# The edge sum's loop on VectorE: 32 steps instead of 56, the last 24 in line, and block numbers read one word at a time

## The reference, cut to what matters

```python
agg  = segment_sum(x[src], dst, n)                  # and the degree of each node
x    = layernorm(x + relu([x, agg/deg] @ W_fc + b_fc) + x @ W_res + b_res)
conv = lambda h: (segment_sum(h[src] @ Wm + bm + edge_attr @ We + be, dst, n) + h @ Ws + bs)
x    = layernorm(x + conv2(relu(conv1(x))))
```

## Time and profile before

| | |
|---|---|
| median of three runs | 3635.19 us |
| profiled execution | 3643.39 us, of it 3641.6 us span |
| VectorE busy, whole span | 2379.0 us (65%) |
| TensorE busy, whole span | 3127.8 us (86%) |
| mark, line 930 | 728 times, 483 ns each |
| add, line 941 | 728 times, 279 ns each |

### The profile page before, as it was taken

How to read it: one execution, slowest core, us unless ns; L and a number is a source line. 1 busy time by engine, 2 the same in 40 slices (tenths; PEclk the granted TensorE clock), 3 DMA queues, 4 the chain that set the end, 5 groups by cost and what they waited for, 6 DMA issues and landing times.

```text
span 3641.6 us, 114539 instructions
## 1 busy us (share of the span) xinstructions
PE 3127.8 (86%) x38568; PEld 2925.0 (80%) x38568; DVE 2379.0 (65%) x6286; ACT 1579.8 (43%) x2164; POOL 2104.5 (58%) x2436
## 2 busy tenths in 40 slices
PE   0228999999999999788888888999999979999995
PEld 0127988888888888677777888999999879999995
DVE  8679998988888888687788664333333333333335
ACT  0123677778999899677777632000000210000000
POOL 5761345455666666333333227777777677777774
PEclk9869999999999999899999859999999999999998
DMA  3521445555666666577777517999999679999995
GB/s 90 136 19 54 181 184 210 205 223 217 246 244 236 237 249 247 192 220 212 208 215 217 155 61 291 399 381 389 397 386 398 236 294 400 385 384 398 390 389 225
DMA packets 234074, 928.58 MB, mean 255 GB/s; under 512 B 46723, under 2 KB 146193, under 8 KB 178030
## 3 DMA queue, kind: packets, MB, share of 16 engines
q1 hardware_dynamic: 182559, 846.33, 62.2%
q0 software_dynamic: 51392, 80.97, 7.7%
HBM read 676.56 MB, written 250.56 MB: 255 GB/s over the span
## 4 chain that ended last, share of the span: by engine, by line
PE 48%; POOL 16%; issue 15%; DVE 11%; DMA 6%; DVEq 3%; ACT 2%; ACTq 0%; POOLq 0%; SPq 0%
PE ps L1118 30%; POOL msg L1280 10%; PE ps L1141 7%; DVE union L814 5%; PE ps L1188 5%; DMA msg<-y_tab,idx 4%; POOL abuf L1222 3%; PE ps L1110 3%; DVE union L930 2%; ACT union L1428 1%; DVE abuf L941 1%; POOL union L1222 1%; PE ps L1197 1%; DVEq L469 1%; PE ps L1078 1%
## 5 line engine op out<-in xcount | busy, mean ns | idle before, releaser
L1280 POOL DMA_INDIRECT msg<-y_tab,idx x1512 | 1614.4, 1068 | 921.5 <-issue 456.4
L1118 PE MATMUL ps<-union,abuf 128*128 128x192 bf16 x14112 | 1210.7, 248 | 14.7 <-DVEq L785 10.2
L1118 PEld LDWEIGHTS ps<-union,abuf 128*128 128x128 f16 x14112 | 1177.4, 99 | 18.5 <-issue 10.6
L1410 ACT ACTIVATE abuf<-ps 128x784 f16<-128x784 f32 x1152 | 949.1, 824 | 262.1 <-PE ps L1141 237.2
L814 DVE TENSOR_TENSOR union<-lane,union 128x1568 f16<-128x1568 f16 (+1 forms) x1384 | 911.9, 710 | 8.4 <-PE ps L1141 4.7
L1118 PE MATMUL ps<-early,abuf 128*128 128x195 bf16 x7154 | 809.3, 249 | 0.0
L1118 PEld LDWEIGHTS ps<-early,abuf 128*128 128x128 f16 x7154 | 641.9, 99 | 92.1
L1141 PE MATMUL ps<-union 128*128 128x98 f16 (+2 forms) x4192 | 661.3, 287 | 57.4 <-DVE union L814 56.3
L1386 ACT ACTIVATE idx<-src_g 128x7 int32 (+1 forms) x216 | 44.4, 205 | 1258.8 <-PE ps L1110 1248.1
L1188 PE MATMUL ps<-union 128*64 128x128 f32 x7280 | 467.7, 287 | 92.6 <-ACT union L1428 89.9
L1188 PEld LDWEIGHTS ps<-union 128*64 128x64 f32 x7280 | 421.1, 144 | 139.3 <-DVE abuf L941 121.8
(11 more groups left out here) (231 smaller groups left out, 1386.5 us busy)
## 6 DMA issues: line engine op xcount, KB each, us to landing
abuf<-a_dram SPq DMA_DIRECT2D x288, 1568.0 KB
a_dram<-abuf SPq DMA_DIRECT2D x72, 3136.0 KB
union<-in_edge_attr_dram SPq DMA_DIRECT2D x728, 160.0 KB, 3.1
msg<-y_tab,idx POOLq DMA_INDIRECT x1512
y_tab<-union SPq DMA_DIRECT2D x28, 336.0 KB, 2.2
abuf<-in_x_dram SPq DMA_DIRECT2D x28, 224.0 KB, 3.6
y_tab<-early SPq DMA_DIRECT2D x7, 682.5 KB, 5.5
out_dram<-union SPq DMA_DIRECT2D x2, 800.0 KB, 3.5
```

Source lines behind the costliest of these rows:

```text
L1118: last = nc.tensor.matmul(ps[:, bank, 0:3 * width_of[r]], abuf[:, buffer, hi * P:(hi + 1) * P], ycols[r][:, hi, :], start=hi == 0, stop=hi ...
L1280: pool.indirect_dma_start(msg[:, s, 0:3 * width_of[r]], None, y_tab[r], bass.IndirectOffsetOnAxis(ap=idx[:, s:s + 1], axis=0)).then_inc(ga ...
L1410: A.activation(abuf[:, j, :].rearrange("p (h w d) -> p w h d", w=WPB, d=WD) [:, w:w + 2, :, :], ps[:, w % 4:w % 4 + 2, 0:WIN].rearrange("p ...
```

## The change

A new constant `HELD` = 4. The steps of the loop go into a function that is called twice: in a loop of 22 passes with 4 turns (32 steps), and once more, with constants in place of the loop's register, for the 3 turns (24 steps) that are left. Block numbers are loaded one word at a time, in every fourth step, and the load stands behind the mark of its step and ahead of the waits of the add, where before it stood ahead of the mark. Nothing on the other engines is edited; SyncE keeps its 56 steps in a pass.

```diff
+    HELD = 4
...
-                with dve.Fori(0, ESTEPS // EB, TURNS) as turn:
-                    for n in range(EB * TURNS):
+                def edge_steps(turn, turns):
+                    for n in range(EB * turns):
                         i, h = turn + n // EB, n % EB
-                        if n % (2 * EB) == 0:
-                            bs = load_blocks(turn * (EB // 4) + (first_block + n) // 4, min(2 * EB, EB * TURNS - n))
                         if h % 2 == 0:
                             dve.wait_ge(e_hot[h // 2], i + 1)
                         dve.wait_ge(e_rel[h], i + 1)
...
                         if h % 2:
                             marks.then_inc(e_mark[h // 2], 1)
+                        if n % 4 == 0:
+                            bs = load_blocks(turn * (EB // 4) + (first_block + n) // 4, 4)
                         b = (h - LAG) % EB
                         dve.wait_ge(e_mm[b], i + (2 if h >= LAG else 1))
                         dve.wait_ge(e_add, i * EB + (h + EB))
-                        to = flat(sums_e[:, bass.ds(bs[n % (2 * EB)], 1), :])
+                        to = flat(sums_e[:, bass.ds(bs[n % 4], 1), :])
                         V.tensor_tensor(to, to, ps[:, b, 0:P], ALU.add).then_inc(e_add, 1)
+
+                whole = ESTEPS // EB // HELD * HELD
+                with dve.Fori(0, whole, HELD) as turn:
+                    edge_steps(turn, HELD)
+                edge_steps(whole, ESTEPS // EB - whole)
```

## The result

The kernel after the change takes 3542.4 us (median of four runs: 3540.2, 3561.2, 3543.9, 3540.8) against 3635.8 us of the kernel before, measured beside it. The ratio is 0.9754, 95% interval 0.9721 to 0.9788: 93 us faster.

What follows compares the result with a forecast made beforehand. VectorE's sequencer was taken to bound the edge sum; 437 us of steps + 44 loads + 7.6 branches + 5 restart and stalls = 493.6 against 552.1, 58.5 less, giving 3576 us; range given 3546 to 3609.

Steps and rivals of the forecast that it cites:

- What bounds the kernel: Edge sum, 552.1 us: VectorE sets the pace at 0.60 us a step, and its own sequencer stops it for 115 us.
- The held loop: Edge loop on VectorE: about 210 instructions stay held, so 36 us of branch pauses go and 21 branches cost 7.6 us.
- restart and inner stalls: Edge sum: clock recovery after pauses, chain refilling and short issue stalls; 5 us of the 37 remain.
- The load term: Edge loop: 182 one-word loads between mark and add at 0.24 us each, 44 us against 42 before.
- Restart and the branch: Edge sum: 5 us kept for restart and inner stalls, 7.6 us for 21 branches at 0.36 us each.
- The sum: Edge sum: 437 + 44 + 7.6 + 5 = 493.6 us against 552.1, 58.5 less.
- Not held: Edge loop: the 32-step body is fetched again at 21 branches, 124 us in place of 5, kernel 3696 us; 7%.
- Load waits for the mark: Edge loop: each load waits until the mark is through, add 0.70 us late, 127 us, kernel 3660 us; 5%.
- Loads hidden: Edge loop: the mark covers the loads at no cost, stage 450 us, kernel 3533 us; 6%.
- What would show it: Edge sum: no 4 us idle ahead of marks, clock 1.00 from second pass, loaded steps 0.64 us mark to add, "issue" moved.

Runs made afterwards that it cites:

- the loop alone: Kernel before with only the 32-step loop, keeping the old loads of up to four words ahead of the mark: 3563.0 us, ratio 0.9801.
- the moved loop of 48: Changed kernel with 48 steps a pass (309 instructions) and the body's start shifted to another slot in the instruction stream: 3540.4 us, ratio 0.9750.
- the announced branch: Kernel before, 56 steps kept, with only the loop's branch target announced at the top of each pass: 3552.2 us, ratio 0.9782.
- the early address: Changed kernel with the address operation of the next load in the loop issued one step earlier: 3541.0 us, ratio 0.9734.
- the two kernels with the filler: 14 useless TensorE products added during the wait ahead of the fold: on the kernel before 3619.2 us, on the changed kernel 3541.5 us.
- load ahead of the mark: Changed kernel with its one-word loads moved from behind the mark to ahead of it: 3575.7 us, ratio 0.9837.
- loop of 40: Changed kernel with 40 steps a pass in place of 32 (258 instructions): 3557.3 us, ratio 0.9777.
- loop of 48: Changed kernel with 48 steps a pass in place of 32 (309 instructions), start not moved: 3628.1 us, ratio 0.9972.

## Why the prediction was right in kind and 34 us off

**What bounds the kernel**: right. VectorE's sequencer set the pace, through the load ahead of the mark and the pause at the branch. Both were tried alone, and each gave a gain.

**The held loop**: right. The forecast took 36 us of branches and 32 of restart and inner stalls off and put 7.6 back, 60.4 in all; the loop alone measured 57.5. That the pause is fetched code was argued from one other loop; the moved loop of 48 and the announced branch show it. The reason given, that 210 instructions are about what is held, was too coarse: 360 are held if they start at the right place, and 309 are not if they don't. (The counts of 209 and 291 that it compared were short, as it said; the trace has 244 in the first passes of line 828's loop and 340 in the edge loop.) The Trainium skill, Runtime: NRT & Kernel Launch, section Instruction fetch mechanics, has a branch out of the window of code stall the engine; here the trace agrees, with 3 us. Its pages of 256 instructions do not fit the stalls, which stand 128 apart, nor the five packets; the rule that the prediction drew from it, that a body which crosses a page is lost, does not hold either, since all bodies that are held cross the end of a block.

**The load term**: the step that failed. It was sized 0.24 us a load and measured 0.13. The terms in the sum were right, but the start was not. The chain of waits after, through the step with the load (start, length, what; DVEq is the sequencer):

```profile
1702.66 0.31 DVEq L470
1702.97 0.09 DVE union L929
...
1703.11 0.04 DVEq L942
...
1703.19 0.06 DVEq L942
...
1703.29 0.30 DVE abuf L942
```

The load begins at 1702.66, 0.10 *ahead* of its mark's start at 1702.76, and its address 0.19 ahead. The forecast had the sequencer hand over the mark 0.07 ahead of its start, and the load so begin 0.02 behind it. The difference is 0.12, nearly all of the step from 0.24 to 0.13. In the trace the step before a load has only one register operation ahead of its add, since the byte that it uses is the last of its word; the other steps have three or four. At the start of a pass the lead is missing, as the same view shows:

```profile
1720.74 0.10 DVE union L929
...
1720.87 0.30 DVEq L470
```

There the load begins 0.13 behind its mark, and mark to add takes 0.79, 0.39 more than in a step without a load. With the early address the load begins 0.20 ahead of its mark and costs 0.04. So with starts 0.20 ahead, 0.10 ahead and 0.13 behind, a load costs 0.04, 0.13 and 0.39: the sequencer's lead sets its price. The load itself was as forecast, 0.306 us for one word in the median:

```profile
L470 DVEq TENSOR_LOAD <-steps x183: 299/306/529, 1511.1 to 1985.4; - x183
L470 DVEq FUSED_REGOPS  x176: 57/57/75, 1511.0 to 1967.0; - x176
```

The floor of about 600 ns that the Trainium skill, DMA: Bandwidth & Descriptors, section Latency and other measured facts, gives for such a load does not hold here: the longest of these 183 took 529 ns.

**Restart and the branch**: sized 5 and 7.6. Each of 21 branches costs 0.22 us ahead of the mark, and the first load of a pass 0.25 more than the others: 21 x 0.22 + 22 x 0.25 = 10 us. What is left for restart and inner stalls is about 4.

**The sum**: the stage was forecast as 493.6 and measured 474.5. Loads at 0.13 in place of 0.24 (a little less in line) take off about 21, and the branches add about 2; that is the 19 us. The rest of the 34, some 15 us, is the fold, which no step of the forecast held: before's profiled run, on which the sum was made, had the slow fold, and so by their times had most of its runs; three of four of after's had the fast one. So of the 93 us between the medians some 16 are the fold's clock and the other 77 or so are the change's own, as the two kernels with the filler show. With those alone the median would have been about 3558 us, inside the range: that the result fell below its low end is owed to the fold, by luck and not by the mechanism. Why the kernel after meets the fast fold more often is not settled: three variants of it without pauses (load ahead of the mark, loop of 40, address early) met the slow one in the profiled run.

**The rivals**: "Not held" fell; the timeline has no idle time of 3 us at a thirty-second mark. "Load waits for the mark" fell at 0.13 us a load, far from the 0.56 at which it decides. "Loads hidden" is half true: the measured stage lies between its 450 and the forecast's 494, a little nearer to the forecast. That its 3533 us is close to the time measured is owed to the fold.

**What would show it**: the clock was 1.00 from 8 us on to the end of the stage. "Issue" left the mark but did not move to the add (8.6 us before, 7.2 after): where the add comes 0.13 late, the row of its mark, 0.49 long, still covers all but 0.04 of the time up to it. The other engines still wait for VectorE, as the waits after show (us, times, longest).

```profile
PEld ps L1194 <- DVE abuf L942: 75.6, 256, 8.9
ACT union L1434 <- DVE union L929: 35.3, 92, 5.2
```

Of 0.64 from mark to add in every fourth step 0.53 was seen.

## What to carry to other kernels

A loop that is too long for an engine's instruction store shows as the same idle "issue" of microseconds at every taken branch, and as extra packets of its instruction queue; shorten it, move its start, or announce the branch, and count the blocks that it touches, not only its instructions. This was shown on VectorE alone. When you place a load into registers, ask how far the sequencer is ahead at that point: the same one-word load cost 0.21, 0.13 or 0.04 us here. Compare a stretch that runs at two clocks apart from the change before you credit the change with it.

## What the runs showed of the hardware that was not expected

- Code comes to VectorE in packets of 8.2 KB, with short stalls 128 instructions apart; a loop that touches three such blocks is held and one that touches four is fetched again at each branch, with five packets and 3.2 to 5.5 us from add to mark, unless the branch is announced. Why it is five packets, and why the announced one is not fetched again, is open.
- With a wait of 1.3 us ahead of it, the fold's 196 products took 40 to 41 us in five profiles and 22 in five others; 14 products in the wait kept it at 22 us in each of the three profiles with it, and none of the 15 runs with it lies apart from the others of its kernel by the 15 us and more seen without it.
- Two of the early-address kernel's four runs, and one of the loop of 40's, were 17 to 23 us faster than the others of the same kernel, and five of the loop of 48's ten some 15 to 26; that this is the fold in each is inferred from the size, since one run of each was profiled.
